# A dense product spread over the next pair's counting groups, and two DRAM copies moved into the first stage

## The chip, the cores and the metric

The kernel runs on one core of a Trainium2 chip. The metric is the device time of one execution in microseconds (us); the median of three runs of the kernel before is 1141.66 us (1140.97 to 1142.63). The engines are PE (TensorE), DVE (VectorE), ACT (ScalarE), POOL (GpSimd) and SP, which only issues DMAs here. Each executes its own instructions in program order and waits on semaphores.

## The reference

Two graph networks on 1250 nodes and 20000 edges (sorted by `dst`), each followed by a residual and a layer norm.

```
# first network, x [1250, 1024]
h = relu(layernorm(x, ln_in_g, ln_in_b) @ W1 + b1)      # 1024 -> 512
h = h @ W2 + b2                                         # 512 -> 256
for i in range(3):
    z = h + segment_sum(h[src], dst)                    # = (A + I) @ h, A[d, s] = number of edges s -> d
    z = relu(z @ Wa[i] + ba[i]) @ Wb[i] + bb[i]
    h = h + relu(layernorm(z, ng[i], nb[i]))
x = layernorm(x + layernorm(x + relu(h @ Wd1 + bd1) @ Wd2 + bd2, out_g, out_b))
# second network: two SAGE layers, h @ W_self + mean of neighbours @ W_neigh + b, 1024 wide
x = layernorm(x + sage(x))
```

The kernel never gathers. It counts the edges into the turned matrix A once and multiplies by it as a dense matrix.

## The kernel before, in words

Four stages follow each other, with a barrier between them: `graph_block`, `encoder_block`, `decoder_block`, `sage_block`. The change touches the first two.

**graph_block** builds A and the first dense product. Nodes come in 10 tiles of 125, worked in PAIRS = 5 pairs; a pair has GROUP = 5 windows of 50 target nodes. For a window DVE makes one-hot masks of a chunk of edges (`visit`: `hot_src` 125x125, `hot_keys` 125x500, into a ring of RING = 12 slots), and PE multiplies the two (`count`) into the window's own PSUM bank. Six chunks per window are counted in a loop over groups j = 0 to 4, then `more` does a number of further rounds that depends on the data (one per pair here): PE chooses the edges of one more chunk (`choose`, L568), DVE takes them (`tab`, L413), PE counts. After that a seventh, last mask for each group closes the bank. ACT copies the counts out (`read_counts`, ten activations, L262), and SP stores the two tiles of A in DRAM (L221).

Beside this the same engines do the dense product z1 = relu(layernorm(x) @ W1 + b1) of the pair. SP loads the rows (`load_rows`, L211), DVE takes their statistics (`statistics`, L365 to L375) and the rest of the scale (`normalizer`, L63 to L381), ACT scales (`normalize`, L236), PE transposes (`turn_norm(p, u)`, 8 transposes, L553), ACT applies gain and bias and rounds to the high half (`affine(p, u)`, L245 and L250), and DVE makes the low half (`norm_low(p, u)`, L421). `dense(p)` (L596) then does 4 column tiles m of 24 matmuls each, in banks 7, 5, 6, 7; the transposes use banks 5 and 6, and `choose` of `more` uses bank 7. ACT takes each tile out (`relu(p, m)`, L270), rounds (L311), and DVE makes the low half (`z1_low(p)`, L427).

PE's order in a pair p before the change: `turn_norm(p, 1)`, five groups of six counts, `more`, five last counts, `turn_norm(p+1, 0)`, `dense(p)` whole. DVE's: the masks of group 0 and 1, `norm_low(p, 0)`, of group 2 and 3, `norm_low(p, 1)`, of group 4, the masks of `more`, the last five masks, `statistics(p+2)`, `z1_low(p-1)`, `normalizer(p+2)`.

**encoder_block** starts with h @ W2 (72 matmuls, L1024), then one transpose of the degrees (L1139), then the products g with the first layer's Wa (60 matmuls, L1024). The weights of these products come in units: SP loads a unit into `w_f32` (L739), POOL rounds it (L762) and makes the low half (L764). ACT issues, as the first thing it does in this stage, two DMAs that copy x in DRAM to `x_bd` and `x_ob` (L893); POOL waits for them later, ahead of the 20 accumulating DMAs that add a bias row to each, and the decoder reads the sums. SP's own order in this stage is: wait for the stores of A, load the degrees' part of A, three bias rows (L734), then the first weight unit.

Of the kernel before, what the change touches and what calls it, by code (L numbers as in the profile page):

```python
# [6 lines left out]
ACT = mybir.ActivationFunctionType  # L7
# [7 lines left out]
N, E = 1250, 20000  # L15
D, H, B, LAYERS = 1024, 512, 256, 3
NT = 125
# [22 lines left out]
def raw(ap):  # L40

    return ap.bitcast(F32)
# [65 lines left out]
def graph_block(nc, block, sem, io, s):  # L108
# [85 lines left out]
    @block.sync  # L194
    def _(sp):
        sp.dma_start(dst_i[0:EP, :, :].rearrange("p j e -> p (j e)"), io["dst_chunks"]).then_inc(dst_in, 16)
        sp.dma_start(src_i[0:EP, :, :].rearrange("p j e -> p (j e)"), io["src_chunks"]).then_inc(src_in, 16)
        sp.dma_start(visit_ids[0:1, :, :].rearrange("p g v -> p (g v)"), io["visit_ids"]).then_inc(visit_in, 16)
        sp.dma_start(iota[:, :], io["iota"]).then_inc(visit_in, 16)
        sp.dma_start(offsets[:, :, :, :].rearrange("p q g v -> p (q g v)"), io["key_offsets"].to_broadcast([128, 2 * VW]))\  # L200
          .then_inc(visit_in, 16)
        for to, name in ((s.ln_gb[:, :, :], "ln_gb"), (s.biases[:, :], "biases")):
            sp.dma_start(to, io[name]).then_inc(consts_in, 16)
        for n in range(KD // 2 + 1):
            unit = io["W1_pairs"][n, :, :] if n < KD // 2 else io["w_units"][0, :, :]
            sp.dma_start(w_f32[n][:, :], unit).then_inc(w_in[min(n // 2, 1)], 16)
        def load_rows(p):
            for u in range(2):
                sp.wait_ge(xhat_ready, 2 * p + u - 1)
                t = 2 * p + u  # L210
                sp.dma_start(x_rows[u][:, :], io["x"][t * NT:t * NT + 128, :]).then_inc(x_in[u], 16)  # L211

        load_rows(1)
        for p in range(PAIRS):
            if p + 2 < PAIRS:
                load_rows(p + 2)
            sp.wait_ge(counts_out, 2 * GROUP * (p + 1))
            if p >= 2:
                sp.wait_ge(eye_added, 2 * (p - 1))
            for t in (2 * p, 2 * p + 1):  # L220
                sp.dma_start(io["at_dram"][t, :, :, :], raw(s.at_[:, :, t * NT:(t + 1) * NT])).then_inc(at_stored[p % 2], 16)  # L221
        s.at_landed = [(at_stored[u], 32 * ((PAIRS + 1 - u) // 2)) for u in range(2)]

    @block.scalar
    def _(act):
        def take_root(p):
            act.wait_ge(var_ready, p + 1)
            act.activation(root[0:NT, :], var_eps[0:NT, :], ACT.Sqrt).then_inc(root_ready, 1)

        def normalize(p, u):  # L230
            t = 2 * p + u
            act.wait_ge(norm_ready, p + 1)
            act.wait_ge(x_in[u], 16 * (p + 1))
            if p > 0:
                act.wait_ge(xhat_read, t - 1)
            act.activation(xhat[u][0:NT, :], x_rows[u][0:NT, :], ACT.Identity, bias=shift[0:NT, u:u + 1],  # L236
                           scale=rstd[0:NT, u:u + 1]).then_inc(xhat_ready, 1)
# [28 lines left out]
        def relu(p, m):  # L266
            act.wait_ge(z1_mm, KH * p + m + 1)
            if m == 0 and p > 0:
                act.wait_ge(z1_split, p)
            act.activation(z1_f32[:, m, :], ps_z1[m][:, 0:2 * NE], ACT.Relu,  # L270
                           bias=s.biases[:, m:m + 1]).then_inc(z1_relu, 1)

        act.dma_start(s.ident[:, :], io["ident"]).then_inc(table_in, 16)
        act.dma_start(table[0:EP, :], io["range_table"]).then_inc(table_in, 16)
        for u in range(2):
# [7 lines left out]
        affine(0, 0)  # L283
        for n in range(2, KD // 2):
            w1_high(n)
        for p in range(PAIRS):
            affine(p, 1)
            if p == 0:
                take_root(1)
                normalize(1, 0)  # L290
            if p + 1 < PAIRS:
                normalize(p + 1, 1)
            if p == 0:
                w1_high(KD // 2)
            if p + 2 < PAIRS:
                take_root(p + 2)
            if p + 1 < PAIRS:
                affine(p + 1, 0)
            read_counts(p)
            relu(p, 0)  # L300
            relu(p, 1)
            if p + 2 < PAIRS:
                normalize(p + 2, 0)
            relu(p, 2)
            relu(p, 3)
            act.wait_ge(z1_relu, KH * (p + 1))
            if p == 0:
                act.wait_ge(w_ready, KD // 2 + 1)
                act.wait_ge(tab_ready, 1)
            for h, t in tile_halves(p):  # L310
                hi = act.activation(s.wide[:, 0, :, t * NT:(t + 1) * NT], z1_f32[:, :, h * NE:h * NE + NT], ACT.Copy)  # L311
            hi.then_inc(z1_hi, 1)

    @block.gpsimd
    def _(pool):
# [45 lines left out]
    def _(dve):  # L361
# [145 lines left out]
        for p in range(PAIRS):  # L507
            for j in range(GROUP):
                for v in range(STATIC - 1):
                    visit(n, GROUP * p + j, v)  # L510
                    n += 1
                if j == 1:
                    if p == 0:
                        w1_low(1)
                    norm_low(p, 0)
                if j == 3:
                    norm_low(p, 1)
                if p == 0:
                    if j == 2:
                        statistics(1)  # L520
                        w1_low(2)
                        w1_low(3)
                    if j == 3:
                        normalizer(1)
            if p == 0:
                dve.wait_ge(trips_known, PAIRS + 1)
            last_trip = dve.value_load(trips_i[0:1, p:p + 1], min_val=p + 2, max_val=(C - STATIC) * (p + 1) + 1)
            more(p, first_trip, last_trip)
            first_trip = last_trip
            for j in range(GROUP):  # L530
                visit(n, GROUP * p + j, STATIC - 1)
                n += 1
            if p + 2 < PAIRS:
                statistics(p + 2)
            if p == 0:
                w1_low(KD // 2)
            else:
                z1_low(p - 1)
            if p + 2 < PAIRS:
                normalizer(p + 2)  # L540
        z1_low(PAIRS - 1)

    @block.tensor
    def _(pe):
# [36 lines left out]
                                   start=False, stop=False)  # L581
                mm.then_inc(more_free, 1)

        def dense(p):
            pe.wait_ge(xt_split, 2 * p + 2)
            if p == 0:
                pe.wait_ge(w_ready, KD // 2)
            own = slice(p % 2, p % 2 + 2)
            for m in range(KH):
                if m == 3:  # L590
                    pe.wait_ge(z1_relu, KH * p + 1)
                if m in (1, 2) and p + 1 < PAIRS:
                    pe.wait_ge(xt_affine, KD * (2 * p + 2) + 4 * m)
                for k in range(KD):
                    for q, (a, b) in enumerate(HALVES):
                        mm = pe.matmul(ps_z1[m][:, 0:2 * NE], w1[:, a, k, m * 128:(m + 1) * 128],  # L596
                                       xt[:, own, b, k, :], start=(k == 0 and q == 0), stop=(k == KD - 1 and q == 2))
                mm.then_inc(z1_mm, 1)

        pe.sem_inc(more_free, 1)  # L600
        pe.sem_inc(more_tab, 1)
# [17 lines left out]
        n, first_trip = 0, 1  # L619
        turn_norm(0, 0)  # L620
        for p in range(PAIRS):
            if p > 0:
                turn_norm(p, 1)
            for j in range(GROUP):
                if p > 0:
                    pe.wait_ge(counts_out, GROUP * (2 * p - 1) + j + 1)
                for v in range(STATIC - 1):
                    count(n, j, v == 0, False)
                    n += 1
                if p == 0 and j == 1:  # L630
                    turn_norm(0, 1)
            if p == 0:
                pe.wait_ge(trips_known, PAIRS + 1)
            last_trip = pe.value_load(trips_i[0:1, p:p + 1], min_val=p + 2, max_val=(C - STATIC) * (p + 1) + 1)
            more(p, first_trip, last_trip)
            first_trip = last_trip
            for j in range(GROUP):
                count(n, j, False, True)
                n += 1
            if p + 1 < PAIRS:  # L640
                turn_norm(p + 1, 0)
            dense(p)


def encoder_block(nc, block, sem, io, s):
# [19 lines left out]
        sem("b_norm"))  # L665
    b_stats, b_var = sem("b_stats"), sem("b_var")
    t_mm, t_out, h_added, h_hi, h_ready = sem("t_mm"), sem("t_out"), sem("h_added"), sem("h_hi"), sem("h_ready")
    x_copied, x_summed = sem("x_copied"), sem("x_summed")

    at = Map(nc, s.stage_at)  # L670
    w_f32 = at("w_f32", [128, 1024], F32)
# [85 lines left out]
    def _(pool):  # L757
# [34 lines left out]
        for n in range(1, UNIT_B1):  # L792
# [1 line left out]
            if FREED[n]:  # L794
                pool.wait_ge(w_free, FREED[n])
            halves(n, SLOT[n])
        pool.wait_ge(x_copied, 32)
        for t in range(T):
            for to, row in (("x_bd", "bd2"), ("x_ob", "out_b")):
                pool.dma_start(io[to][t * NT:(t + 1) * NT, :], io[row].to_broadcast([NT, D]), accum_op=ALU.add)\  # L800
# [9 lines left out]
    def _(act):  # L810
# [78 lines left out]
            for t in range(7, T):  # L889
                g(t)  # L890

        for to in ("x_bd", "x_ob"):
            act.dma_start(io[to], io["x"]).then_inc(x_copied, 16)  # L893
        for j in range(ZC):
            act.wait_ge(z_mm, j + 1)
            k, cols = chunk(j)
# [788 lines left out]
def places(nc):  # L1685
# [35 lines left out]
    s.dx_in = [nc.alloc_semaphore(f"dx_in{u}") for u in range(3)]  # L1721
    s.dy_in = [nc.alloc_semaphore(f"dy_in{u}") for u in range(2)]
    s.row_in = nc.alloc_semaphore("row_in")
    s.rows_in = [nc.alloc_semaphore(f"rows_in{u}") for u in range(2)]
    s.bias_in = nc.alloc_semaphore("bias_in")
    s.turned = nc.alloc_semaphore("turned")
# [82 lines left out]
```

## Time and profile before

| | before |
|---|---|
| median of 3 runs | 1141.66 us |
| the profiled execution | 1139.84 us |
| its span, first to last instruction | 1138.0 us |
| PE busy | 1026.1 us |
| mean granted TensorE clock | 0.942 |
| first stage ends at about | 181 us |

The profiled execution is 1.84 us longer than its span; the times of single instructions below are counted from the span's start. A busy PE may be a PE at half clock: the granted clock is given per stretch, 1.00 for 2.4 GHz and 0.50 for 1.2 GHz.

### The profile page before, as it was taken

What the parts mean: (1) busy time and instruction counts of PE and PEld (TensorE: products, weight loads), DVE (VectorE), ACT (ScalarE), POOL (GpSimd) and SP (SyncE); (2) the same over time, 40 slices, a digit from 0 to 9 for tenths busy, and PEclk for the clock granted to TensorE, in tenths of its full rate; (3) what the DMA queues carried; (4) which work ended last, traced back from release to release, by engine and by line L of the source; (5) the groups of instructions that cost most, each with busy time, mean ns of one, the idle gap of its engine ahead of it and who ended that gap; (6) DMA issues with size and microseconds to landing.
All of it is one profiled execution on the core that took longest, in us unless ns stands there. A gap on an engine that the chain in (4) does not pass through costs nothing.

```text
span 1138.0 us, 14851 instructions
## 1 busy us (share of the span) xinstructions
PE 1026.1 (90%) x4862; PEld 824.3 (72%) x4862; DVE 532.1 (47%) x1314; ACT 351.0 (31%) x632; POOL 254.9 (22%) x314
## 2 busy tenths in 40 slices
PE   5799997298988589699999999999999999999996
PEld 2566667187988468577777777778888778777775
DVE  7988852137556658633222233221324332434455
ACT  5454532015243437722111122111342111222222
POOL 3000000184132433170600333300604200500000
PEclk9788888599999889889999999999999999999998
DMA  5144338689200248430422310432441433302534
GB/s 190 39 82 83 46 63 229 213 187 206 63 19 1 111 133 290 171 117 18 131 91 75 126 43 22 148 112 97 135 156 59 142 119 122 116 0 82 164 131 133
DMA packets 48232, 127.13 MB, mean 112 GB/s; under 512 B 17712, under 2 KB 18721, under 8 KB 47953
## 3 DMA queue, kind: packets, MB, share of 16 engines
q1 hardware_dynamic: 33622, 74.91, 22.5%
q0 software_dynamic: 8000, 27.02, 9.4%
q10 hardware_dynamic: 6554, 24.47, 6.3%
q8 instruction: 33, 0.54, 0.2%
q14 instruction: 23, 0.18, 0.1%
HBM read 101.76 MB, written 45.13 MB: 129 GB/s over the span
## 4 chain that ended last, share of the span: by engine, by line
PE 57%; DVE 0%; ACT 0%; issue 0%; DVEq 0%; ACTq 0%
PE bank L1632 39%; PE bank L1653 16%; PE bank L1379 1%; ACT h_rows L1558 0%; DVE f_st L85 0%; DVE h_stage L1580 0%; ACT h_stage L1532 0%; DVE o L1603 0%; DVE f_mv L88 0%; ACT f_rt L1555 0%; DVE f_rs L63 0%; DVE f_sh L95 0%; DVE f_rs L71 0%; DVE f_sc L65 0%; DVE f_sc L67 0%
## 5 line engine op out<-in xcount | busy, mean ns | idle before, releaser
L1580 DVE TENSOR_TENSOR h_stage<-h_turned,h_stage 128x1000 fp32r<-128x1000 f32 x80 | 106.0, 1326 | 382.0 <-ACT h_stage L1532 382.0
L1632 PE MATMUL bank<-w_neigh,h_stage 128*125 128x512 f32 x960 | 228.7, 399 | 4.2 <-DVE h_stage L1580 4.2
L1632 PE MATMUL bank<-w_self,h_stage 128*125 128x512 f32 x960 | 229.5, 394 | 0.0
L1632 PEld LDWEIGHTS bank<-w_neigh,h_stage 128*125 128x125 f32 x960 | 178.9, 187 | 50.0 <-DVE h_stage L1580 4.6
L1632 PEld LDWEIGHTS bank<-w_self,h_stage 128*125 128x125 f32 x960 | 177.9, 185 | 44.9
L1653 PE MATMUL bank<-g_rows,a_stage 125*125 125x512 f32 x800 | 192.2, 394 | 0.0
L1532 ACT ACTIVATE h_stage<-h_turned 128x1000 fp32r (+1 forms) x80 | 83.7, 1048 | 318.0 <-PE bank L1632 304.9
L1653 PEld LDWEIGHTS bank<-g_rows,a_stage 125*125 125x125 f32 x800 | 148.4, 186 | 37.4
L1056 PE MATMUL bank<-a_turned,gn 125*128 125x418 f32 x360 | 70.5, 354 | 2.9 <-DVE gn L918 2.9
L1494 POOL CAST w_self<-w_stage 128x512 fp32r<-128x512 f32 x32 | 20.2, 632 | 233.1 <-PE bank L1632 220.6
L1056 PEld LDWEIGHTS bank<-a_turned,gn 125*128 125x128 f32 x360 | 67.0, 188 | 4.4 <-DVE gn L918 3.6
L560 PE MATMUL bank<-hot_keys,hot_src 125*128 125x500 bf16 x175 | 55.4, 438 | 15.5 <-DVE hot_keys L390 14.4
L1353 PE MATMUL bank<-w_self,wide 128*125 128x512 f32 x240 | 59.3, 405 | 2.1 <-PEq L1788 2.1
L390 DVE TENSOR_SCALAR hot_keys<-iota,tab 125x500 bf16<-125x500 f16 x175 | 60.9, 348 | 0.0
L596 PE MATMUL bank<-xt,w 128*128 128x252 f32 x480 | 58.6, 283 | 0.0
L596 PEld LDWEIGHTS bank<-xt,w 128*128 128x128 f32 x480 | 57.6, 190 | 0.4 <-issue 0.3
L560 PEld LDWEIGHTS bank<-hot_keys,hot_src 125*128 125x128 bf16 x175 | 18.6, 106 | 50.4 <-DVE hot_keys L390 34.6
L1353 PEld LDWEIGHTS bank<-w_self,wide 128*125 128x125 f32 x240 | 45.1, 191 | 13.5 <-issue 2.7
L389 DVE TENSOR_SCALAR hot_src<-iota,tab 125x125 bf16<-125x125 f16 x175 | 45.8, 262 | 19.1 <-PE bank L560 18.5
L1024 PE MATMUL bank<-weight_slots,ht 128*125 128x256 f32 x180 | 29.1, 326 | 23.8 <-POOL weight_slots L764 20.5
L1603 DVE SCALAR_TENSOR_TENSOR o<-bank,deg_inv,o 125x512 f32<-125x512 f32 x40 | 30.0, 751 | 35.8 <-PE bank L1653 33.6
L1024 PEld LDWEIGHTS bank<-weight_slots,ht 128*125 128x125 f32 x180 | 27.0, 227 | 25.5 <-POOL weight_slots L764 20.6
(200 smaller groups left out, 1117.6 us busy)
## 6 DMA issues: line engine op xcount, KB each, us to landing
a_stage<-at_dram SPq DMA_DIRECT2D x40, 625.0 KB, 4.1
w_stage<-w_self POOLq DMA_DIRECT2D x32, 256.0 KB, 3.2
at_dram<-a_turned SPq DMA_DIRECT2D x10, 625.0 KB, 9.6
w_stage<-w_neigh POOLq DMA_DIRECT2D x24, 256.0 KB, 3.0
dec_y<-x_bd SPq DMA_DIRECT2D x10, 512.0 KB, 4.1
dec_x<-x_ob SPq DMA_DIRECT2D x10, 512.0 KB, 4.7
x_dram<-h_rows SPq DMA_DIRECT2D x10, 512.0 KB, 3.2
h_dram<-o ACTq DMA_DIRECT2D x20, 256.0 KB
```

Source lines behind the costliest of these rows:

```text
L389: dve.tensor_scalar(hot_src[0:EC, slot, 0:NT], iota[0:EC, 0:NT], tab[0:EC, 1, g, v:v + 1], None, ALU.is_equal)
L390: dve.tensor_scalar(hot_keys[0:EC, slot, :], iota[0:EC, :], tab[0:EC, 0, g, v:v + 1], None, ALU.is_equal)\
L560: mm = pe.matmul(ps_counts[j][:, 0:KEYS], hot_src[0:EC, slot, :], hot_keys[0:EC, slot, :], start=start, stop=stop)
L596: mm = pe.matmul(ps_z1[m][:, 0:2 * NE], w1[:, a, k, m * 128:(m + 1) * 128], xt[:, own, b, k, :], start=(k == 0 and q == 0), stop=(k == KD ...
L1024: mm = pe.matmul(out, w(a, k), x(b, k), start=(k == 0 and p == 0), stop=(k == k_tiles - 1 and p == 2))
L1056: mm = pe.matmul(ps_z[j % 2][:, 0:CH], cast(gn[0:NT, h, k, m * 128:(m + 1) * 128]), cast(s.at_[0:NT, k, cols]), start=(k == 0 and h == 0), ...
L1353: mm = pe.matmul(banks[2 * (t % 2) + c][0:NT, :], s.wide[:, a, k, t * NT:(t + 1) * NT], s.w_self[:, b, k * D + 512 * c:k * D + 512 * c + 512],
L1532: act.activation(st[u][:, 0, :, :], ht[:, :, cols], ACT.Copy).then_inc(st_hi, 1)
L1580: dve.tensor_tensor(st[u][:, 1, :, :], ht[:, :, bass.ds(t * NT, NT)], raw(st[u][:, 0, :, :]), ALU.subtract).then_inc(st_ready, 1)
L1603: dve.scalar_tensor_tensor(out=o[u][0:NT, :], in0=ps_a[u][0:NT, :], scalar=s.deg_inv[0:NT, bass.ds(t, 1)], in1=o[u][0:NT, :], op0=ALU.mult ...
L1632: mm = pe.matmul(out, st[u][:, a, k, :], w[:, b, k * 512:(k + 1) * 512], start=(k == 0 and p == 0), stop=(k == KD - 1 and p == 2))
L1653: mm = pe.matmul(ps_a[u][0:NT, :], cast(a_st[u][0:NT, k, :]), cast(g[0:NT, h, k, :]), start=(k == 0 and h == 0), stop=(k == T - 1 and h == 1))
```

## The change

`dense` takes one column tile m. PE does tile m of pair p-1 ahead of group j = m of pair p, for j = 0 to 3, and `turn_norm(p, 1)` moves from the head of pair p to behind tile 3. Only the last pair's product is still done whole, at the end. ACT's order follows: `read_counts(p-1)` comes first in its round p, `affine(p, 1)` and `normalize(p+1, 1)` last. On DVE `norm_low(p, 0)` moves behind group 2's masks, `norm_low(p, 1)` behind the pair's last masks (ahead of `statistics(p+2)`), and `normalizer(p+1)` behind group 0's masks of pair p. The two copies of x leave ACT in the encoder; SP issues them in the first stage instead, in thirds of 418, 418 and 417 rows, each third behind the stores of A of pair 0, 1 and 2.

```diff
@@ graph_block, sync: after the stores of pair p
+            own = slice(p * CH, min((p + 1) * CH, N + 128 - NT))
+            for to in ("x_bd", "x_ob") if p < NCH else ():
+                sp.dma_start(io[to][own, :], io["x"][own, :]).then_inc(s.x_copied, 16)
@@ graph_block, scalar
+        affine(0, 1)
+        take_root(1)
+        normalize(1, 0)
+        normalize(1, 1)
+        w1_high(KD // 2)
+        for p in range(1, PAIRS):
+            read_counts(p - 1)
+            if p + 1 < PAIRS:
+                take_root(p + 1)
+            affine(p, 0)
+            relu(p - 1, 0)
+            relu(p - 1, 1)
+            if p + 1 < PAIRS:
+                normalize(p + 1, 0)
+            relu(p - 1, 2)
+            relu(p - 1, 3)
+            z1_high(p - 1)
             affine(p, 1)
             if p + 1 < PAIRS:
                 normalize(p + 1, 1)
+        read_counts(PAIRS - 1)
+        for m in range(KH):
+            relu(PAIRS - 1, m)
+        z1_high(PAIRS - 1)
@@ graph_block, vector: behind the six masks of group j
-                if j == 1:
-                    if p == 0:
+                if p == 0:
+                    if j == 1:
                         w1_low(1)
-                    norm_low(p, 0)
-                if j == 3:
-                    norm_low(p, 1)
+                        norm_low(0, 0)
...
+                else:
+                    if j == 0 and p + 1 < PAIRS:
+                        normalizer(p + 1)
+                    if j == 2:
+                        norm_low(p, 0)
@@ behind the last five masks
+            if p > 0:
+                norm_low(p, 1)
             if p + 2 < PAIRS:
                 statistics(p + 2)
             if p == 0:
                 w1_low(KD // 2)
             else:
                 z1_low(p - 1)
-            if p + 2 < PAIRS:
-                normalizer(p + 2)
@@ graph_block, tensor
-            if p > 0:
-                turn_norm(p, 1)
             for j in range(GROUP):
                 if p > 0:
+                    if j < KH:
+                        dense(p - 1, j)
+                    if j == KH - 1:
+                        turn_norm(p, 1)
                     pe.wait_ge(counts_out, GROUP * (2 * p - 1) + j + 1)
...
             if p + 1 < PAIRS:
                 turn_norm(p + 1, 0)
-            dense(p)
+        for m in range(KH):
+            dense(PAIRS - 1, m)
@@ encoder_block, gpsimd and scalar
-        pool.wait_ge(x_copied, 32)
+        pool.wait_ge(s.x_copied, 16 * 2 * NCH)
...
-        for to in ("x_bd", "x_ob"):
-            act.dma_start(io[to], io["x"]).then_inc(x_copied, 16)
```

## Rows read from the trace of the kernel before

**Rows 1.** Timeline of PE, start of encoder; columns: start, duration, instruction, idle before and releaser.
```profile
201.43 0.37 PE L1139 MATMUL bank<-ident,degrees 10*125 10x10 f32 x1 [4.10 <-DVE degrees L1001]
222.28 5.22 PE L1024 MATMUL bank<-weight_slots,ht 128*125 128x256 f32 x24 [20.48 <-POOL weight_slots L764]
```

**Rows 2.** Timelines of POOL and of SP's queue, start of encoder.
```profile
219.89 2.34 POOL L764 TENSOR_TENSOR weight_slots<-w_f,weight_slots 128x1024 fp32r<-128x1024 f32 x1
...
184.21 45.88 SPq L739 DMA_DIRECT2D w_f<-w_units  x3
```

**Rows 3.** DMA issues, 176 to 222 us: KB each, median us from issue to landing.
```profile
x_ob<-x ACTq DMA_DIRECT2D x1, 5012.0 KB, 35.4
w_f<-w_units SPq DMA_DIRECT2D x1, 512.0 KB, 34.4
```

**Rows 4.** Windows: length, busy (instructions) per engine, PE clock, DMA share, GB/s; encoder.
```profile
204.00:206.00 2.00, 0.00 (x0) 0.00 (x0) 0.00 (x0) 0.00 (x0) 0.00 (x0) 0.50 0.97 328
```

**Rows 5.** Windows of the first stage, cut where PE starts to choose (L568).
```profile
41.36:70.41 29.05, 26.59 (x161) 19.03 (x161) 25.05 (x100) 15.44 (x37) 1.09 (x2) 0.91 0.56 104
70.41:100.33 29.92, 27.92 (x161) 19.44 (x161) 25.36 (x103) 15.45 (x37) 1.09 (x2) 0.84 0.48 79
100.33:130.41 30.08, 28.07 (x161) 19.81 (x161) 25.03 (x102) 15.66 (x37) 0.87 (x2) 0.84 0.31 44
130.41:159.36 28.95, 26.52 (x160) 19.04 (x161) 21.48 (x90) 13.21 (x34) 1.14 (x2) 0.91 0.32 45
```

**Rows 6.** Timeline of PE, one cycle of the first stage.
```profile
77.31 11.58 PE L596 MATMUL bank<-xt,w 128*128 128x252 f32 x96
88.73 1.02 PE L553 MATMUL bank<-ident,xhat 125*128 125x125 f32 x8
89.58 6.02 PE L560 MATMUL bank<-hot_keys,hot_src 125*128 125x500 bf16 x24
96.84 0.37 PE L560 MATMUL bank<-hot_keys,hot_src 125*128 125x500 bf16 x1 [1.24 <-DVE hot_keys L390]
...
100.33 0.98 PE L568 MATMUL bank<-more_pick,edge_keys 80*125 80x5 f32 x4 [0.42 <-issue]
...
102.00 2.24 PE L580 MATMUL bank<-more_keys,more_src 125*128 125x500 bf16 x5
```

**Rows 7.** Timeline of DVE, the same cycle's start.
```profile
72.33 0.18 DVE L413 TENSOR_TENSOR tab<-bank,offsets 125x10 f32<-125x10 f32 x1 [0.31 <-PE bank L568]
...
74.65 2.47 DVE L365 BATCH_NORM_STATS2 stats<-x_rows 125x6 f32<-125x512 f32 x4
...
77.54 1.26 DVE L427 TENSOR_TENSOR wide<-z_f,wide 128x500 fp32r<-128x500 f32 x2
...
79.71 0.16 DVE L381 SCALAR_TENSOR_TENSOR shift<-mean_var,rstd 125x2 f32<-125x2 f32 x1
...
84.86 1.20 DVE L421 TENSOR_TENSOR xt<-xt_f,xt 128x1000 fp32r<-128x1000 f32 x1
90.00 0.26 DVE L389 TENSOR_SCALAR hot_src<-iota,tab 125x125 bf16<-125x125 f16 x1 [3.94 <-PE bank L560]
```

**Rows 8.** Timeline of ACT, the same cycle.
```profile
81.62 2.79 ACT L262 ACTIVATE a_turned<-bank  x10
...
90.47 2.86 ACT L245 ACTIVATE xt_f<-bank,ln_gb 128x125 f32<-128x125 f32 x8
...
94.31 1.23 ACT L236 ACTIVATE xhat<-x_rows,shift,rstd 125x1024 f32<-125x1024 f32 x1
```

**Rows 9.** Windows: the microseconds in which PE's granted clock falls and rises.
```profile
97.00:98.00 1.00, 0.82 (x2) 0.10 (x1) 1.00 (x5) 0.00 (x0) 0.67 (x2) 0.67 0.59 197
...
107.00:108.00 1.00, 1.00 (x8) 1.00 (x7) 0.93 (x5) 0.31 (x2) 0.00 (x0) 0.71 0.00 0
```

**Rows 10.** DMA issues, 40 to 80 us.
```profile
x_rows<-x SPq DMA_DIRECT2D x3, 512.0 KB, 4.3
at_dram<-a_turned SPq DMA_DIRECT2D x2, 625.0 KB, 9.9
```

More of the change, by code:

```diff
@@ L271, in relu, with z1_high @@
                            bias=s.biases[:, m:m + 1]).then_inc(z1_relu, 1)
+        def z1_high(p):
+            act.wait_ge(z1_relu, KH * (p + 1))
+            if p == 0:
+                act.wait_ge(w_ready, KD // 2 + 1)
+                act.wait_ge(tab_ready, 1)
+            for h, t in tile_halves(p):
+                hi = act.activation(s.wide[:, 0, :, t * NT:(t + 1) * NT], z1_f32[:, :, h * NE:h * NE + NT], ACT.Copy)
+            hi.then_inc(z1_hi, 1)
         act.dma_start(s.ident[:, :], io["ident"]).then_inc(table_in, 16)
@@ L285, in _ @@
             w1_high(n)
-        for p in range(PAIRS):
+        affine(0, 1)
[15 more added lines that the diff above has]
+            z1_high(p - 1)
             affine(p, 1)
-            if p == 0:
-                take_root(1)
-                normalize(1, 0)
             if p + 1 < PAIRS:
                 normalize(p + 1, 1)
-            if p == 0:
-                w1_high(KD // 2)
-            if p + 2 < PAIRS:
[L296 to L312, printed above, removed]
+        read_counts(PAIRS - 1)
+        for m in range(KH):
+            relu(PAIRS - 1, m)
+        z1_high(PAIRS - 1)
     @block.gpsimd
@@ L511, in _ @@
                     n += 1
-                if j == 1:
-                    if p == 0:
+                if p == 0:
+                    if j == 1:
                         w1_low(1)
-                    norm_low(p, 0)
-                if j == 3:
-                    norm_low(p, 1)
-                if p == 0:
+                        norm_low(0, 0)
                     if j == 2:
@@ L523, in _ @@
                     if j == 3:
+                        norm_low(0, 1)
                         normalizer(1)
+                else:
[3 more added lines that the diff above has]
+                        norm_low(p, 0)
             if p == 0:
@@ L538, in _ @@
                 z1_low(p - 1)
-            if p + 2 < PAIRS:
-                normalizer(p + 2)
         z1_low(PAIRS - 1)
@@ L582, in more, with dense @@
                 mm.then_inc(more_free, 1)
[L584 to L587, printed above, removed]
-            own = slice(p % 2, p % 2 + 2)
[L589 to L598, printed above, removed]
+        def dense(p, m):
+            if m == 0:
+                pe.wait_ge(xt_split, 2 * p + 2)
+                if p == 0:
+                    pe.wait_ge(w_ready, KD // 2)
+            own = slice(p % 2, p % 2 + 2)
+            if m == 3:
+                pe.wait_ge(z1_relu, KH * p + 1)
+            if m in (1, 2) and p + 1 < PAIRS:
+                pe.wait_ge(xt_affine, KD * (2 * p + 2) + 4 * m)
+            for k in range(KD):
+                for q, (a, b) in enumerate(HALVES):
+                    mm = pe.matmul(ps_z1[m][:, 0:2 * NE], w1[:, a, k, m * 128:(m + 1) * 128],
+                                   xt[:, own, b, k, :], start=(k == 0 and q == 0), stop=(k == KD - 1 and q == 2))
+            mm.then_inc(z1_mm, 1)
         pe.sem_inc(more_free, 1)
@@ L667, in encoder_block @@
     t_mm, t_out, h_added, h_hi, h_ready = sem("t_mm"), sem("t_out"), sem("h_added"), sem("h_hi"), sem("h_ready")
-    x_copied, x_summed = sem("x_copied"), sem("x_summed")
+    x_summed = sem("x_summed")
     at = Map(nc, s.stage_at)
@@ L1723, in places @@
     s.row_in = nc.alloc_semaphore("row_in")
+    s.x_copied = nc.alloc_semaphore("x_copied")
     s.rows_in = [nc.alloc_semaphore(f"rows_in{u}") for u in range(2)]
```

## The prediction

> **What bounds the kernel now.** The page says PE is busy 1026 of 1138 us, so I looked for the places where PE is idle or slow, and first at the list of waits of the first 235 us. The two largest PE entries there lead to the timelines. At the start of the encoder PE finishes h @ W2 at 197.4 us, waits 4.1 us for the degrees, does one transpose at 201.43, and then stands for 20.48 us until 222.28; the releaser named is POOL's low half of a weight unit [rows 1]. POOL makes that half at 219.89 and itself waited for a DMA; SP issued the load at 184.21 [rows 2]. The DMA view gives the load of 512 KB 34.4 us from issue to landing, and beside it ACT's copy of x, 5012 KB, with 35.4 us [rows 3]. While nothing computes, the DMA engines are 0.97 busy at 328 GB/s [rows 4]: the load of one weight unit is starved by the two copies that ACT issued at 181. This stall, and not the first stage, is the large item.
>
> In the first stage I cut the time where PE begins to choose, once per pair. The four cycles last 29.05, 29.92, 30.08 and 28.95 us, 118.0 together; PE is busy 26.5 to 28.1 of each and DVE 21.5 to 25.4 [rows 5]. Neither bounds a cycle alone: DVE stands 3.94 us while the ring is full and PE does the dense product [rows 7], then PE waits 1.24 us for masks, counts as slowly as DVE makes them, and falls to half clock just behind that (0.67 over the microsecond at 97, 0.71 over the one at 107 in which it returns) [rows 6, 9]. At half clock five counts take 2.24 us, against 6.02 us for 24 at full [rows 6], so 1.0 us more for these alone.
>
> **The copies.** Removed from the encoder: both. Then SP's load, issued 3.2 us into the stage, meets only the small loads issued just ahead. The x_rows loads of the same size took 4.3 us [rows 10]; I allow 4 to 10. POOL needs 3.4 us (219.89 + 2.34 less its start at 218.8) [rows 2], so the unit is ready 11 to 17 us into the stage (192 to 198 on the old time line), and PE asks for it at 201.8, behind the transpose [rows 1]. What is late next is the degrees' sum, whose 4.1 us wait stays. Gain: 222.28 - 201.8 = 20.5 us. The products g behind it start at half clock in both kernels (5.22 us for the first 24, [rows 1]), so nothing is won there. The next two units are loaded and split while PE does the 9.6 us of g, as now; the accumulating DMAs keep their place behind them.
>
> Added to the first stage: six DMAs on SP's queue of 1.71 MB, 3.42 MB behind each of the first three stores. At the old rate (10.26 MB landed in 35.4 us, [rows 3]) a pair of them takes 11.8 us. Behind them stand the x_rows loads of pair p+3, and behind those the next stores. Stores (9.9 us, [rows 10]) and copies fill some 23 us of a 28 us cycle. The stores of A only have to be in before the stage ends, 60 us later, so only the x_rows loads matter: see below.
>
> **The order in the first stage, by PE and DVE.** At full clock the work of PE in a cycle is: dense 11.4 (four tiles of 2.85), two sets of transposes 1.7, 30 counts at 0.25 = 7.5, choose with its issue 0.4 + 1.7 [rows 6]. After choosing, DVE makes the last five masks (72.33 to 74.65, [rows 7]), so PE ends its last count 2.6 us after choosing. Sum 25.3 us if PE never waits.
>
> Now DVE behind choosing, in a cycle with statistics, counted from the end of choosing: last masks until 2.5, norm_low(p, 1) 1.1, statistics 2.9, z1_low 1.2 (74.65 to 77.54 to 78.7) [rows 7], so the first mask of the next group 0 starts at 7.75 and the sixth is there at 10.3. PE meanwhile: last count 2.6, transposes 3.45, tile 0 of the dense product 6.3, and then it waits for those masks: group 0 ends at 10.4 instead of 7.8. From there PE never waits (tiles 1 to 3, groups 1 to 4, transposes, choose: 3 x 2.85 + 4 x 1.5 + 0.85 + 2.1 = 17.5), as DVE makes six masks in 2.5 us, a tile and a group take PE 4.35, and the normaliser (1.1 us to 79.8, [rows 7]) and norm_low(p, 0) fit between. Cycle: 27.9. The last cycle has no statistics: DVE starts group 0 at 4.85 and PE does not wait: 25.3. The first has the statistics but no norm_low(0, 1) behind the masks: 26.7.
>
> ACT: read_counts 2.8, affine with its copy 3.8, four relus, the rounding and again 3.8 + 1.2 [rows 8] stay under 20 us of a cycle. One result of its order is late: normalize(p+1, 1) now comes behind affine(p, 1), which comes behind PE's tile 3 and the transposes. PE ends these 3.6 + 1.5 us or so ahead of the cycle's end; transposed rows out, copied and normalised is 5.1 us [rows 8]. So x_rows of tile (p+2, 1) is asked for at about the end of the cycle, lands 4.3 us later [rows 10], 2.6 us after choosing has ended at best, while DVE wants it at 4.8. Behind a copy still running it lands later: for pair 3 I get copies done at about 73 us and DVE asking at 73 to 75, with the load in by 76 to 77. I take 2.3 us of wait for pair 3 and 0.8 for pair 4; bounds 0 and 6 for each (no copy in the way, and half a copy pair).
>
> The granted clock is the unknown. In all four old cycles it falls behind an idle of about 1.2 to 1.6 us followed by counting at DVE's pace, and comes back after 6 to 10 us. That place vanishes (PE has a full ring in groups 3 and 4), but a new one of the same kind appears: in the cycles with statistics PE waits 1.5 to 4 us behind tile 0 and then counts group 0 at DVE's pace. If the clock falls there, a tile and a group run at half speed: price 0 to 3 us a cycle, as a tile of 2.85 us takes twice that and five counts 1.0 us more; below zero it can't be, since the sums above are at full clock. I take 1 us in each of the four, nearer to the five counts than to the tile: 27.7, 31.2, 29.7, 26.3, sum 114.9. That is 3.1 us less than 118.0. Both ends: 107.8 with no wait and no fall (10.2 less), 121 with these waits and 2.5 us of slow clock in every cycle (3 more). PE's tail behind the last choosing stays at 17.5 us: norm_low(4, 1) now delays dense(4) to 3.6 us after choosing, as late as the last counts and transposes did. The rest of the kernel has no instruction changed.
>
> Sum: 20.5 + 3.1 = 23.6 us. On the profiled execution's own 1139.84 us that is 1116.2; the median shown is 1.8 us above that execution, which gives 1118.0.
>
> **Rivals.**
> (a) The first stage gains in full. For it: PE's idle and slow places of today all lie behind one long dense product; against: the 2.6 us gap counted above. Cycles 107.8: 20.5 + 10.2 = 30.7, so 1111.0.
> (b) The first stage loses: the clock falls in the new gap as well as behind choosing, and statistics wait for x_rows behind the copies. Cycles 121: 20.5 - 3 = 17.5, so 1124.2. For it: DMA engines full for 23 of 28 us.
> (c) The stall is not the copies': the unit is late for another reason (the bias rows just ahead of it in SP's queue landed as late). Then only 3.1 us are won: 1138.6. Against: landing times of load and copies agree, 34.4 and 35.4 [rows 3].
> (d) Slower. If a copy's share among the DMA engines went by its rows, 418 = 2 x 11 x 19 would give 11 engines and 417 = 3 x 139 only 3. At 0.29 MB/us on 16 engines [rows 3], 3 engines move 0.054: the third pair's 3.42 MB takes 63 us, from 116 to 179 us, and the stores of A of pairs 3 and 4 (9.9 us each, [rows 10]) stand behind it until 199. The stage can't end before they are in and POOL has added the diagonal, at 200.5 instead of 178: 22.5 us lost, and 10 more for x_rows behind copies of 17 us: 1118.0 + 32.5 = 1150.5. It decides when that copy pair takes over 41 us. Against: a copy of 1253 = 7 x 179 rows would have had 7 engines, a share of 0.44, and the row shows 0.97 [rows 4].
> The Trainium skill (DMA: Bandwidth & Descriptors, "Why a DMA increments its semaphore by 16 and not by 1") has this rule, the largest number up to 16 that divides the slowest dimension; the trace disagrees for the whole copy, which suggests that it was issued in another shape, and no row shows the thirds.
>
> **Chances.** Forecast 0.55, (a) 0.18, (b) 0.18, (c) 0.04, (d) 0.03, other 0.02. The range reaches from just below (a) to just over (b)'s middle: 1110 to 1124. About 0.2% (2.3 us) is what a measurement of this kernel can tell from no change: faster 0.95, same 0.02, slower 0.03.
>
> **What would show it.** PE's idle ahead of its first g product gone, and w_f landing in under 10 us; copies of 1.7 MB landing in 6 to 12 us each; PE idle 1.5 to 4 us behind tile 0 in the two cycles with norm_low and statistics and nearly none ahead of choosing; DVE no longer idle on the ring. Wrong if the stall stays, if the granted clock in 41 to 155 us is under 0.8, or if the cycles sum to under 108 or over 121.

## The result, and the profile after

The changed kernel takes 1111.1 us (1106.8 to 1113.1, four runs) against 1142.1 (four runs of the kernel before): ratio 0.9725, 95% interval 0.9695 to 0.9755. The forecast was 1118.0 with a range of 1110 to 1124; the measured time lies in it, just above its lower end and at rival (a)'s 1111.0. The gain is 31.0 us where 23.6 were forecast. Two executions of more than 1600 us, one of e6 and one of the kernel before beside it, are in no number below. The profiled execution's span fell from 1138.0 to 1109.3 us, by 28.7. Three cuts place it, on the start of the encoder's first product, on the first g product, and on the end:

| stretch | before | changed | difference |
|---|---|---|---|
| start to the encoder's first matmul | 181.1 | 171.1 | -10.0 |
| from there to the first g product | 41.2 | 22.8 | -18.4 |
| from there to the end | 915.7 | 915.5 | -0.3 |

The timeline of PE after, at the encoder's start, answers to [rows 1]. Columns are start, duration, instruction, and idle before with its releaser:

```profile
171.09 15.47 PE L1037 MATMUL bank<-wide,weight_slots 128*128 128x418 f32 x72 [4.26 <-POOLq L805]
193.54 0.37 PE L1152 MATMUL bank<-ident,degrees 10*125 10x10 f32 x1 [6.97 <-DVE degrees L1014]
193.85 5.08 PE L1037 MATMUL bank<-weight_slots,ht 128*125 128x256 f32 x24
```

The 20.48 us of idle ahead of the g products are gone, and the wait for the degrees one line above has grown from 4.10 to 6.97. The DMA issues of the encoder's start (KB each, median us to landing) show the weight units landing in 3.6 us, where the first one took 34.4 before [rows 3]:

```profile
w_f<-w_units SPq DMA_DIRECT2D x3, 512.0 KB, 3.6
```

In the first stage the windows are cut where PE begins to choose, as in [rows 5] (length, busy per engine, granted PE clock, DMA share, GB/s):

```profile
42.19:67.87 25.68, 25.64 (x160) 19.44 (x161) 24.86 (x104) 12.84 (x32) 1.08 (x2) 0.88 0.83 159
67.87:98.89 31.02, 25.59 (x162) 19.30 (x160) 25.86 (x104) 15.66 (x38) 1.00 (x2) 0.89 1.01 247
98.89:126.84 27.95, 24.91 (x162) 18.62 (x160) 25.22 (x101) 15.66 (x38) 1.07 (x2) 0.94 0.89 188
126.84:150.29 23.45, 23.32 (x161) 18.17 (x160) 21.43 (x88) 14.33 (x36) 1.18 (x2) 1.00 0.39 56
```

The four cycles sum to 108.1 us in place of 118.0. Three got shorter; the second is longer than before (31.02 against 29.92). Why, the timelines of PE and then of DVE in that cycle show:

```profile
72.48 3.10 PE L608 MATMUL bank<-xt,w 128*128 128x252 f32 x24
80.87 2.66 PE L572 MATMUL bank<-hot_keys,hot_src 125*128 125x500 bf16 x6 [5.30 <-DVE hot_keys L399]
82.98 4.40 PE L608 MATMUL bank<-xt,w 128*128 128x252 f32 x24
87.22 1.45 PE L572 MATMUL bank<-hot_keys,hot_src 125*128 125x500 bf16 x6
```

```profile
71.24 1.18 DVE L430 TENSOR_TENSOR xt<-xt_f,xt 128x1000 fp32r<-128x1000 f32 x1
75.69 1.29 DVE L374 BATCH_NORM_STATS2 stats<-x_rows 125x6 f32<-125x512 f32 x2 [3.27 <-DMA x_rows<-x]
77.33 1.29 DVE L374 BATCH_NORM_STATS2 stats<-x_rows 125x6 f32<-125x512 f32 x2 [0.35 <-DMA x_rows<-x]
...
79.04 1.26 DVE L436 TENSOR_TENSOR wide<-z_f,wide 128x500 fp32r<-128x500 f32 x2
80.22 0.25 DVE L398 TENSOR_SCALAR hot_src<-iota,tab 125x125 bf16<-125x125 f16 x1
```

After norm_low DVE stands 3.27 us for the rows of pair 3, which SP asked for behind the first third of the copies; the masks of group 0 start only at 80.22, and PE is idle for 5.30 us. The granted clock falls in that gap, so group 0 and part of the next tile run at half clock, and the tile takes 4.40 us instead of some 3.15:

```profile
77.00:78.00 1.00, 0.00 (x0) 0.00 (x0) 0.67 (x2) 0.00 (x0) 0.00 (x0) 1.00 1.28 173
79.00:80.00 1.00, 0.00 (x0) 0.00 (x0) 1.00 (x3) 0.83 (x4) 0.00 (x0) 0.50 1.32 96
```

The other tiles and groups of this cycle run with no wait. Cycle 3 has a gap of 2.90 us at the same place, cycles 1 and 4 have none.

### The profile page after: what moved, and what is told of

Same layout as the page of the kernel before. It is cut to its first block, busy times and chain, and to the rows that moved or that the text cites. A ratio compares the mean times of both kernels' runs of the same rounds, so it can differ in the third digit from the quotient of the medians.

```text
span 1109.3 us, 14855 instructions
## 1 busy us (share of the span) xinstructions
PE 1013.9 (91%) x4862; PEld 820.1 (74%) x4862; DVE 533.4 (48%) x1314; ACT 351.8 (32%) x632; POOL 254.6 (23%) x314
## 4 chain that ended last, share of the span: by engine, by line
PE 58%; DVE 0%; ACT 0%; issue 0%; DVEq 0%; ACTq 0%
PE bank L1645 40%; PE bank L1666 17%; PE bank L1392 1%; ACT h_rows L1571 0%; DVE f_st L85 0%; DVE h_stage L1593 0%; ACT h_stage L1545 0%; DVE o L1616 0%; DVE f_mv L88 0%; ACT f_rt L1568 0%; DVE f_rs L63 0%; DVE f_sh L95 0%; DVE f_rs L71 0%; DVE f_sc L67 0%; DVE f_sc L65 0%
## 5 line engine op out<-in xcount | busy, mean ns | idle before, releaser
L1593 DVE TENSOR_TENSOR h_stage<-h_turned,h_stage 128x1000 fp32r<-128x1000 f32 x80 | 103.4, 1294 | 383.4 <-ACT h_stage L1545 383.4
L572 PE MATMUL bank<-hot_keys,hot_src 125*128 125x500 bf16 x175 | 53.0, 427 | 17.0 <-DVE hot_keys L399 16.2
L608 PE MATMUL bank<-xt,w 128*128 128x252 f32 x480 | 64.1, 292 | 0.7 <-DVE xt L430 0.7
L608 PEld LDWEIGHTS bank<-xt,w 128*128 128x128 f32 x480 | 60.6, 194 | 2.7 <-DVE xt L430 1.0
L830 ACT ACTIVATE act_out<-bank,biases 128x418 f32<-128x418 f32 x30 | 18.0, 608 | 81.2 <-PE bank L1069 62.4
L1509 POOL TENSOR_TENSOR w_self<-w_stage,w_self 128x512 fp32r<-128x512 f32 x32 | 41.3, 1289 | 2.7
## 6 DMA issues: line engine op xcount, KB each, us to landing
at_dram<-a_turned SPq DMA_DIRECT2D x10, 625.0 KB, 10.4
```

What stands on the lines that cost most here:

```text
L572: mm = pe.matmul(ps_counts[j][:, 0:KEYS], hot_src[0:EC, slot, :], hot_keys[0:EC, slot, :], start=start, stop=stop)
L1509: pool.tensor_tensor(lo, w_f32[u][:, :], raw(hi), ALU.subtract).then_inc(w_ready, 1)
L1593: dve.tensor_tensor(st[u][:, 1, :, :], ht[:, :, bass.ds(t * NT, NT)], raw(st[u][:, 0, :, :]), ALU.subtract).then_inc(st_ready, 1)
```

## Experiments

Ten experiments ran, one of them (e5) the changed kernel again. Cycles are the four intervals between PE's starts of choosing; "stage" is the start of the encoder's first matmul; the waits are PE's, ahead of the degrees' transpose and of the first g product. Both come from the profiled execution of each kernel. The ratio compares means with the runs of the kernel before that were taken beside each kernel, so it differs a little from the quotient of two medians.

| kernel | cycles, us | stage | wait degrees / unit | median, ratio to before (95%) |
|---|---|---|---|---|
| before | 29.1 29.9 30.1 29.0 | 181.1 | 4.1 / 20.5 | 1142 |
| changed | 25.7 31.0 28.0 23.5 | 171.1 | 7.0 / 0 | 1111.1, 0.9725 (0.9695 to 0.9755) |
| e1 copies only | 28.6 37.5 33.9 30.3 | 194.0 | 7.0 / 0 | 1136.5, 0.9964 (0.9952 to 0.9976) |
| e2 order only | 25.7 27.7 29.0 23.4 | 168.5 | 4.1 / 20.0 | 1127.0, 0.9870 (0.9852 to 0.9888) |
| e3 copies elsewhere | 25.7 28.4 27.9 23.5 | 167.4 | 7.0 / 0 | 1108.2, 0.9716 (0.9702 to 0.9730) |
| e4 one copy left | 29.9 30.0 29.7 30.0 | 184.2 | 4.1 / 4.6 | 1126.1, 0.9852 (0.9826 to 0.9878) |
| e5 changed again | 26.0 29.9 28.8 23.4 | 171.3 | 7.0 / 0 | 1110.7, 0.9720 (0.9705 to 0.9736) |
| e6 old order, copies elsewhere | 30.3 28.8 29.4 30.7 | 183.7 | 7.0 / 0 | 1123.6, 0.9840 (0.9823 to 0.9857) |
| e7 degrees first | 25.7 31.0 27.9 23.4 | 171.9 | 4.1 / 0 | 1107.1, 0.9687 (0.9671 to 0.9703) |
| e8 normalize before affine | 25.7 26.0 26.0 23.5 | 163.9 | 7.0 / 0 | 1105.6, 0.9683 (0.9668 to 0.9698) |
| e9 three edits | 26.0 26.1 26.0 23.5 | 163.9 | 4.1 / 0 | 1102.2, 0.9643 (0.9622 to 0.9663) |
| e10 z1_low later | 26.1 25.5 25.5 23.5 | 162.4 | 4.1 / 0 | 1101.5, 0.9648 (0.9634 to 0.9661) |

**The two halves by themselves.** e1 is the kernel before with SP's thirds and without ACT's copies; e2 is the changed kernel with

```diff
-            own = slice(p * CH, min((p + 1) * CH, N + 128 - NT))
-            for to in ("x_bd", "x_ob") if p < NCH else ():
-                sp.dma_start(io[to][own, :], io["x"][own, :]).then_inc(s.x_copied, 16)
...
+        for to in ("x_bd", "x_ob"):                     # ACT, head of the encoder
+            act.dma_start(io[to], io["x"]).then_inc(s.x_copied, 16)
```

> Only the copies moved (in thirds, behind the stores of A of pairs 0, 1, 2), the order of the dense product as before. My theory: the 20.5 us stall ahead of the first g product is the copies' doing, and in the old order x_rows are asked for some 35 us before their use, so the copies cost the first stage nothing. Gain 18 to 20.5 us, time 1121.5 to 1124; idle of PE ahead of g under 1 us besides the degrees' wait; the four cycles still 118 +- 1 us. Rival (the copies delay the first stage wherever they stand, by their DMA time): cycles 2 and 3 longer by 2 us or more each, gain 14 to 16.

> Only the new order, both copies still issued by ACT in the encoder. My theory: the first stage gains more than the 10 us seen, since the longest cycle (31.0 us) waits for x_rows behind the copies: cycles 25.7, 28, 28, 23.5 = 105, gain 13 to 14 us, time 1128 to 1129.5; DVE waits about 1.3 us for x_rows in each of cycles 2 and 3, PE idles 2.5 to 3 us there. Rival (x_rows are late only by ACT's order): same cycles as with the copies, 108, gain 10, time 1132. The 20.5 us stall in the encoder stays by both.

e1 won about 4 us by its ratio (2.7 to 5.5) and 5.5 between the medians, not 18 to 20.5: my theory fell, and its rival too, whose price was far too small. The encoder gave 18.5 (its first g product comes 22.6 us after the stage's end, in place of 41.2), but the first stage lost 12.9 (194.0 against 181.1). The timelines of DVE, of ACT and of PE in its second cycle:

```profile
80.98 2.53 DVE L368 BATCH_NORM_STATS2 stats<-x_rows 125x6 f32<-125x512 f32 x4 [6.21 <-DMA x_rows<-x]
```

```profile
84.07 0.20 ACT L231 ACTIVATE root<-var_eps 125x2 f32<-125x2 f32 x1 [17.80 <-DVE var_eps L378]
84.18 2.87 ACT L248 ACTIVATE xt_f<-bank,ln_gb 128x125 f32<-128x125 f32 x8
87.08 1.04 ACT L253 ACTIVATE xt<-xt_f 128x1000 fp32r<-128x1000 f32 x1
88.02 2.79 ACT L265 ACTIVATE a_turned<-bank  x10
```

```profile
85.71 11.22 PE L599 MATMUL bank<-xt,w 128*128 128x252 f32 x72 [4.96 <-ACT xt_f L248]
```

The rows come 6.21 us late, ACT's root waits for the statistics, the affine stands behind the root, and PE's tile 1 waits 4.96 us for the affine; read_counts is behind both. e2 won 15 us, a little more than I expected: its stage ends 12.6 us earlier (168.5), the stall of 20.0 stays. So the parts are not additive: 4 to 5.5 and 15 us alone, 31 together. The copies cost the first stage 12.9 us in the old order and 2.6 in the new one (171.1 against 168.5). In the new order ACT reads the counts first, so SP issues the first stores at 50.3 us instead of 56.0 and the copies behind them as much earlier; the rows are in at 75.7 instead of 81.0, while DVE asks at 72.4 instead of 74.8. A wait of 3.3 us is left of 6.2. Only both orders as wholes were compared; which part of the new order shortens the wait was not tested by itself.

**Is it the copies' bytes that stall the encoder?** e4 keeps the old order, leaves x_bd's copy on ACT and moves only x_ob's:

```diff
-        for to in ("x_bd", "x_ob"):
-            act.dma_start(io[to], io["x"]).then_inc(x_copied, 16)
+        act.dma_start(io["x_bd"], io["x"]).then_inc(s.x_copied, 16)
```

> The old order; the copy to x_ob moved into the first stage in thirds, the copy to x_bd still issued by ACT in the encoder. My theory: the stall follows the bytes in the way. One copy of 5012 KB takes 17 to 20 us, the weight unit lands 16 to 20 us after its issue in place of 34.4, POOL needs 3.4 more, so PE idles 0 to 4 us ahead of g in place of 20.5: gain 16 to 20 us, time 1122 to 1126. Rival (a fixed delay of the queue, or the bias rows ahead of the unit): the unit still lands after 30 us or more, stall 17 to 20, time 1139 to 1142.

PE waits 4.6 us in place of 20.5, a little over the upper bound; the unit lands after 19.2 us in place of 34.4, and the bias rows just ahead of it after 18.8 where the kernel before showed 33.6. The copy itself takes 20.0. So with half the bytes in the way the unit is held up about half as long, and PE, which asks for it only some 18 us after its issue, sees little of that. The thirds of the other copy cost the first stage 3.1 us here (184.2 against 181.1):

```profile
x_bd<-x ACTq DMA_DIRECT2D x1, 5012.0 KB, 20.0
...
bb_row<-bb SPq DMA_DIRECT2D x3, 128.0 KB, 18.8
```

**Is it the place of the copies that costs the first stage?** e3 (new order) and e6 (old order) issue the first third behind the first row loads and two thirds behind pair 2's stores:

```diff
+        def copy_x(third):
+            own = slice(third * CH, min((third + 1) * CH, N + 128 - NT))
+            for to in ("x_bd", "x_ob"):
+                sp.dma_start(io[to][own, :], io["x"][own, :]).then_inc(s.x_copied, 16)
+
         load_rows(1)
+        copy_x(0)
         for p in range(PAIRS):
...
+            for third in (1, 2) if p == 2 else ():
+                copy_x(third)
```

> The changed kernel with the first third of the copies behind the first row loads (at about 20 us, where the DMA engines stand idle) and the two others behind the stores of pair 2, when no row load is left. My theory: cycle 2 falls from 31.0 to 27.5 to 28.5 us (DVE's wait for x_rows from 3.6 to 1.4), the others as they were: 3 us less than the changed kernel, 1107.5 to 1109, ratio to before 0.970. Rival (waits are by ACT's order alone): cycle 2 stays at 31, time 1111. A loss is possible if the early copies delay the row loads of pair 2, asked for at about 41 us: then cycle 1 grows by 1 to 3 us.

> Old order; first third of the copies behind the first row loads (about 20 us), two thirds behind pair 2's stores, when no row load is left. My theory: moving the copies won only 5.5 us in the old order because the thirds stood ahead of the row loads of pairs 3 and 4: DVE waited 6.2 and 3.6 us for rows, ACT's square root waited for DVE, the affine behind it for the root, and PE's tile 1 for the affine. Away from the row loads the first stage is back at 118 +- 1.5 us for the four cycles and the encoder's 18.4 us stay: 1122 to 1125. Rival (the copies cost the first stage wherever they stand, by use of the DMA engines or of DRAM): cycles still 125 to 130 us, time 1133 to 1137.

e6 decides it: cycles 119.2 instead of 130.3, 1123.6 us instead of 1136.5, with the same bytes moved. In its four cycles DVE waits for no rows. Cycles 1 and 4 are 1.2 and 1.7 us longer than before; in both PE stays at half clock for longer (granted clock 0.84 and 0.83 in place of 0.91), and whether the copies have a part in that was not tested. In e3 cycle 2 is 28.4 instead of 31.0 and the stage ends 3.7 us earlier, as expected; the time (0.9716 beside 0.9720 for e5 and 0.9725) can't be told from the changed kernel's. In the profiled execution of e3, the slowest of its five (1111.1 us), some 2 us of the gain are gone by the time the decoder starts; why was not followed up.

**The degrees' wait.** e7 adds one line to the changed kernel's encoder:

```diff
             if FREED[n]:
                 pool.wait_ge(w_free, FREED[n])
+            if n == 2:
+                pool.wait_ge(deg_summed, 1)
             halves(n, SLOT[n])
```

> The changed kernel; POOL waits for the sum of the degrees before it splits weight unit 2. My theory: the wait ahead of the degrees' transpose grew from 4.1 to 7.0 us since POOL's split of unit 2 now runs beside DVE's last split, which takes 1.23 + 2.62 us in place of 0.38 + 0.59. With POOL waiting, DVE's last split is back at 0.4 + 0.6 us, the wait at 4.1 to 4.5, gain 2.5 to 2.9 us on the changed kernel; unit 2 is ready by 197, needed at 215. Rival (DVE is slow there for another reason, the DMAs that write the weights): wait stays at 7.0, time unchanged.

Beside it the changed kernel ran again, and came out as at first:

> The changed kernel once more, beside the three below on one chip. Ratio to before 0.971 to 0.975, time 1108 to 1113; cycles 25.7, 31, 28, 23.5; wait for the degrees 7.0 us.

The changed kernel's DVE, and then its POOL, at the last split:

```profile
187.25 1.23 DVE L925 CAST ht<-h_f 128x418 fp32r<-128x418 f32 x1 [1.27 <-ACT h_f L910]
188.51 2.62 DVE L927 TENSOR_TENSOR ht<-h_f,ht 128x418 fp32r<-128x418 f32 x1
191.05 2.44 DVE L1014 TENSOR_REDUCE degrees<-deg_parts 10x125 f32<-10x1250 f32 x1
```

```profile
187.21 1.04 POOL L777 CAST weight_slots<-w_f 128x1024 fp32r<-128x1024 f32 x1 [5.12 <-PEq L1150]
188.33 2.35 POOL L779 TENSOR_TENSOR weight_slots<-w_f,weight_slots 128x1024 fp32r<-128x1024 f32 x1
```

and DVE in e7:

```profile
188.11 0.38 DVE L927 CAST ht<-h_f 128x418 fp32r<-128x418 f32 x1 [1.27 <-ACT h_f L912]
188.52 0.59 DVE L929 TENSOR_TENSOR ht<-h_f,ht 128x418 fp32r<-128x418 f32 x1
```

Each DVE instruction that starts just behind one of POOL's ends 0.2 to 0.5 us after it; without POOL it takes 0.38 and 0.59 us. PE's wait is back at 4.1 us and the kernel 3.7 us faster than e5 beside it (0.9687 against 0.9720, the intervals just apart), where 2.5 to 2.9 was expected. The Trainium skill (SBUF — State Buffer, "Who interferes with whom") has a port pair that these two engines share, and which the one that issues first holds for its whole instruction when DVE's instruction is of a kind that needs it; the trace agrees, 2.62 us in place of 0.59. The rival of the expectation, that the DMAs slow DVE, is answered by the wait itself, which went with POOL's instructions.

**The order of asking.** e8 is e3 with

```diff
             z1_high(p - 1)
-            affine(p, 1)
             if p + 1 < PAIRS:
                 normalize(p + 1, 1)
+            affine(p, 1)
```

> The kernel with the copies elsewhere in the new order (e3), and normalize(p+1, 1) ahead of affine(p, 1) on ACT, so that x_rows of tile (p+2, 1) is asked for 3.9 us earlier. My theory: DVE's wait for rows (1.3 us in each of cycles 2 and 3) goes and PE's idle ahead of group 0's masks falls from 2.9 to 1.6 us: cycles 2 and 3 shorter by 1.3 to 2.5 us each, 2.6 to 4 us less than e3, ratio to before 0.968 to 0.969. Rival: affine(p, 1) ends 1.2 us later, norm_low(p, 1) waits for it, and nothing or up to 1 us a cycle is won; cycle 4 grows by 0 to 1 us.

Both cycles fall to 26.0 us, each within its bound and together 4.3 less than in e3, 0.3 over the 4 named; the fourth is unchanged. The time is 2.7 us less than e3's, and the ratio 0.9683 is the expected one. The PE timeline and the windows of cycles 2 and 3 of e8:

```profile
77.16 2.40 PE L577 MATMUL bank<-hot_keys,hot_src 125*128 125x500 bf16 x6 [1.48 <-DVE hot_keys L404]
```

```profile
67.88:93.90 26.02, 24.26 (x161) 18.06 (x160) 25.21 (x102) 15.69 (x38) 1.10 (x2) 1.00 0.49 90
93.90:119.88 25.98, 24.19 (x162) 17.99 (x161) 25.23 (x102) 15.69 (x38) 1.08 (x2) 1.00 0.93 190
```

The gap ahead of group 0 is 1.48 us, where e3 had 2.78 and 2.86, and the clock no longer falls there (e3: 0.94 over each of the two cycles). The fall is what was won beyond the wait for the rows.

**Together, and one step on.** e9 is e8 with e7's line; e10 also moves z1_low:

```diff
                 else:
+                    if j == 0 and p >= 2:
+                        z1_low(p - 2)
                     if j == 0 and p + 1 < PAIRS:
                         normalizer(p + 1)
...
-            else:
+            elif p == PAIRS - 1:
                 z1_low(p - 1)
```

> The new order with all three edits: the copies elsewhere, normalize ahead of affine, and POOL's split of unit 2 behind the degrees' sum. If the edits act at different places (rows in the first stage, DVE beside POOL in the encoder) they add: e8 less 2.9 us, 1102 to 1104, ratio to before 0.965 to 0.967. If they overlap, e8's time.

> As e9, and z1_low(p-1) behind the masks of the next group 0 instead of ahead of them (the last pair's stays). My theory: PE's idle of 1.5 us ahead of group 0 in cycles 2 and 3 is what DVE has left to do there; 1.2 us of it go: cycles 2 and 3 at 24.8 us in place of 26.0, and cycle 4 the same or 0.3 less; 2 to 2.5 us less than e9, 1099.5 to 1102. Rival: DVE is as full as PE in cycles 2 and 3 (26 of 27 us busy), the 1.2 us come back later as a wait for masks of group 1 or for choosing, and the time is e9's within 1 us.

e9's edits add up: 0.9643, 8 to 9 us below the changed kernel. e10 shows its rival: PE's gap ahead of group 0 falls from 1.45 to 0.28 us, but the counts of group 1 now wait for masks (they take 2.10 us instead of 1.44), and only 0.5 us of the 1.2 stay in each cycle. Its time is e9's. Already in cycles 2 and 3 of e8, above, DVE is busy 25.2 of 26.0 us, so it leaves little to win there.

## Why the prediction was right, and where it was not

The mechanism was right: the stall was the copies' doing, and only the row loads made the copies felt in the first stage. Three sizes were off, in part against each other, so that a gain of 31.0 us came in place of 23.6.

**The stall.** Right, and shown: removed bytes, removed wait (e2 keeps 20.0 us, e4 4.6, the changed kernel 0). I counted 20.5 us, the stage gave 18.4: 20.5, less the 2.9 us by which the degrees' wait grew, plus 0.7 for a shorter h @ W2 (15.47 us against 16.2). "What is late next is the degrees' sum, whose 4.1 us wait stays" failed on its length. I had looked at POOL's new times only for when the unit is ready, not for what DVE does beside POOL.

**The copies in the first stage.** "Only the x_rows loads matter" was right. I took 2.3 us of wait for pair 3 and 0.8 for pair 4; DVE waited 3.6 and 1.3 (2.3 of the first behind the copies: e2 and e3, with none in the way, wait 1.2 to 1.3 in each). That cycle 2 took 31.0 us where 31.2 were forecast is luck: e8 shows 26.0 with neither wait nor fall of the clock, where I had 27.9; the wait was 1.3 longer than I took, and the fall cost 1.4 where I had 1. A repeat of the same kernel (e5) has 29.9 and 28.8 for cycles 2 and 3.

The thirds landed 18.8 to 20.8 us after their issue, not in the 6 to 12 named as a sign:

```profile
x_bd<-x SPq DMA_DIRECT2D x1, 1668.0 KB, 19.3
x_ob<-x SPq DMA_DIRECT2D x1, 1668.0 KB, 20.8
```

Those times hold the stores of A ahead of them in the queue, 10.4 us in the median; what is left agrees, as an estimate, with the 11.8 us of the prediction for a pair.

**The sum of a cycle at full clock.** This term was mis-sized, and it is the largest error. I had 25.3 us of PE work; cycle 4, with no wait and the clock at 1.00 throughout, takes 23.45. Two things of [rows 6] were read at the wrong price. Counts were put at 0.25 us from "24 in 6.02", a stretch in which PE used the ring up and then kept DVE's pace; from a full ring six take 1.1 us start to start. Choosing was put at 2.1 us with its issue, from a stretch at half clock; it takes 0.8 with the clock up. The timeline of PE after, in cycle 4:

```profile
131.45 3.14 PE L608 MATMUL bank<-xt,w 128*128 128x252 f32 x24
134.43 1.45 PE L572 MATMUL bank<-hot_keys,hot_src 125*128 125x500 bf16 x6
135.53 3.23 PE L608 MATMUL bank<-xt,w 128*128 128x252 f32 x24
...
150.29 0.50 PE L580 MATMUL bank<-more_pick,edge_keys 80*125 80x5 f32 x4
150.65 0.58 PE L580 MATMUL bank<-more_pick,edge_src 80*125 80x5 f32 x4
151.09 1.22 PE L592 MATMUL bank<-more_keys,more_src 125*128 125x500 bf16 x5
```

The five groups take 5.8 us in place of 7.5 and choosing 0.8 in place of 2.1, 3.0 less; four tiles of 3.0 in place of 2.85 and last counts until 2.9 in place of 2.6 after choosing take 1.0 back: 23.3, within 0.2 us of the cycle. With it, cycles 2, 3 and 4 were put 1.9 us too long each. Cycle 1, less what the half clock costs it (below), comes to 23.5 us where I had 26.7, 3.2 too long, since the gap behind tile 0 did not come there. That is 8.9 us too much; the waits, 1.8 longer than I took, and the clock, 0.2 dearer, bring it to the 6.9 by which the first stage came out better.

**The clock.** I charged 1 us in each cycle. In cycle 1 PE still chooses and makes the last counts at half clock, as it did before the change, where the same four matmuls at the cycle's start took 1.00 us too:

```profile
42.19 1.00 PE L580 MATMUL bank<-more_pick,edge_keys 80*125 80x5 f32 x4 [0.46 <-issue]
45.92 2.29 PE L572 MATMUL bank<-hot_keys,hot_src 125*128 125x500 bf16 x5
67.87 0.50 PE L580 MATMUL bank<-more_pick,edge_keys 80*125 80x5 f32 x4
```

Against cycle 4 that costs about 2.2 us (25.7 against 23.5). In cycles 2 and 3 (0.89 and 0.94) the clock fell in the gaps of 5.30 and 2.90 us, for about 1.4 and 0.6 us; in cycle 4 it did not fall. So the four together cost some 4.2 us where I had 4.0, each at another price than mine: the sum is luck. The loss behind choosing is gone from cycles 2 to 4, as forecast. Together the first stage gained 10.0 us where I had 3.1, and the two errors, 2.1 too much in the encoder and 6.9 too little here, make up the 4.8 us between the 23.6 forecast and the 28.4 seen between the profiled executions, 1139.84 and 1111.47 us.

The signs: the four cycles sum to 108.1 us, hardly inside the 108 below which I had called the forecast wrong; PE was idle 2.90 us behind tile 0 in one of the two cycles, as named, and 5.30 in the other, over the 4 named; DVE no longer waits for the ring, and PE is not idle ahead of choosing.

**Rival (a)** had the time by luck, not for its reasons: both of its terms were off, 20.5 for an encoder that gave 18.4, and 107.8 with no wait and no fall for cycles that had both. **(b)** was right that statistics wait behind the copies and that the clock falls in the new gap, and wrong that it also falls behind choosing in cycles 2 to 4. **(c)** is ruled out by e4 and by the changed kernel, where the same bias rows and units stand in the same queue. **(d)**, the copies on few DMA engines, was to show itself by a pair that takes over 41 us; the last pair, of 417 rows, landed within 21 us of its issue (above). While it runs the engines move some 390 GB/s, where (d) had worked out 54 for three of them:

```profile
122.00:124.00 2.00, 2.00 (x20) 2.00 (x19) 2.00 (x11) 0.36 (x1) 0.00 (x0) 1.00 1.11 386
```

(The DMA share, 1.11 here and 2.57 between 84 and 85 us, can pass 1, so it says less than the rate and the landing.) The divisor rule that the prediction cites is not borne out for this copy of 417 rows; in which shape it was issued was not looked at.

## What to carry to other kernels

A transfer that is off every path still has a place in a queue: ask which later load stands behind it, when that load is next wanted, and what the waiting engine has behind its wait. Two changes that use the same slack are to be measured apart, since here moving the copies was worth 4 to 5.5 us in one order and 16 in the other. Price an instruction from a stretch in which its inputs were there and the clock was up, never from one in which the engine was fed slowly.

## What the runs showed that was not expected

- A DMA's landing time followed the bytes already under way on another engine's queue: 34.4 us for 512 KB behind 10.3 MB, 19.2 behind 5.1 MB, 3.6 with nothing in the way.
- A wait of 6.2 us for one load made a cycle 7.5 us longer in e1, with PE at a granted clock of 0.78 there, through DVE, ACT and PE in a row.
- A PE gap of 1.5 us followed by a group counted at DVE's pace left the clock at 1.00 in both cycles of e8; gaps of 2.9 and 5.3 us at the same place in the changed kernel brought it to 0.50.
- DVE instructions of 0.38 and 0.59 us took 1.23 and 2.62 us beside two of POOL's.
